# A graph-attention kernel whose odd adjacency halves are issued by another engine

## The reference, cut to what matters

```python
x: (8192, 256) f32;  adj: (8192, 8192) int32, 0 or 1, sparse, denser in the first rows and columns
h = x @ W                                             # W: 256 x 256
e = leaky_relu(s1[:, None] + s2[None, :], 0.2)        # s1 = h @ attn[:256, 0], s2 = h @ attn[256:, 0]
e = where(adj > 0, e, -9e15)
attention = softmax(e, axis=1)
out = layernorm(x + elu(attention @ h))
```

## Time and profile before

| what | value |
|---|---|
| median of 3 runs | 861.21 us (860.45 to 862.23) |
| the profiled execution's own time | 860.82 us |
| its span, first to last instruction | 859.1 us |
| moved by DMA | 320.21 MB |
| mean DMA rate over the span | 373 GB/s |
| busy: PE / DVE / ACT / POOL | 70% / 72% / 67% / 71% |
| granted TensorE clock, mean | 0.883 |

### The profile page before, as it was taken

The page is one execution under the profiler, slowest core; times in us unless marked ns, Lnnn a source line. Parts: engine busy times, 40 slices in busy tenths (PEclk is TensorE's granted clock), DMA queues, the critical chain, the costliest instruction groups (busy, mean ns, idle before and its releaser), DMA issues.

```text
span 859.1 us, 10648 instructions
## 1 busy us (share of the span) xinstructions
PE 598.4 (70%) x2590; PEld 385.8 (45%) x2633; DVE 614.6 (72%) x2385; ACT 577.6 (67%) x531; POOL 607.0 (71%) x695
## 2 busy tenths in 40 slices
PE   5588986646858777586787675777648775786641
PEld 4466662424536445353454343544425353454331
DVE  4257552567688987779897587788858877887863
ACT  3034536668777987878787497686959858897510
POOL 4487425778778777587865888888888786887742
PEclk9799999788978999898898988889889897999966
DMA  8999997999999999999999999999999998999400
GB/s 324 401 399 408 388 382 313 411 419 407 416 376 412 416 418 415 416 418 411 404 398 420 415 382 406 374 362 372 417 402 405 408 416 340 396 416 419 154 23 31
DMA packets 62850, 320.21 MB, mean 373 GB/s; under 512 B 19286, under 2 KB 37943, under 8 KB 46400
## 3 DMA queue, kind: packets, MB, share of 16 engines
q1 hardware_dynamic: 36176, 285.49, 81.7%
q0 software_dynamic: 25456, 29.79, 10.5%
q10 hardware_dynamic: 1152, 4.19, 1.2%
HBM read 344.79 MB, written 17.14 MB: 421 GB/s over the span
## 4 chain that ended last, share of the span: by engine, by line
issue 24%; POOL 20%; DMA 20%; DVE 17%; PE 15%; ACT 2%; POOLq 1%; SPq 0%; ACTq 0%; DVEq 0%
POOL GATH L1474 18%; DMA GATH<-haug,ids 7%; DMA ADJ<-in_adj_dram 6%; PE acc L513 6%; DMA WORK<-in_adj_dram,smalls 3%; DMA X<-in_x_dram 3%; PE pk L527 3%; PE acc L538 3%; DVE GATH L761 2%; ACT WORK L1296 2%; DVE diag L834 2%; PE mid_acc L604 1%; DVE smalls L775 1%; DVE WORK L951 1%; DVE PART L844 1%
## 5 line engine op out<-in xcount | busy, mean ns | idle before, releaser
L1474 POOL DMA_INDIRECT GATH<-haug,ids x448 | 471.5, 1053 | 132.5 <-issue 128.7
L1296 ACT ACTIVATE WORK<-ADJ 128x4096 bf16<-128x4096 int32 x128 | 461.9, 3609 | 138.7 <-PE pk L527 83.5
L527 PE MATMUL pk<-WORK,D 128*128 128x512 bf16 x981 | 256.6, 411 | 129.8 <-ACT WORK L1296 125.9
L527 PEld LDWEIGHTS pk<-WORK,D 128*128 128x128 bf16 x1024 | 100.1, 103 | 264.3 <-ACT WORK L1296 150.2
L538 PE MATMUL acc<-GATH,diag 128*128 128x256 f32 x512 | 157.3, 462 | 80.6 <-DVE diag L834 80.6
L538 PEld LDWEIGHTS acc<-GATH,diag 128*128 128x128 f32 x512 | 117.2, 235 | 123.6 <-DVE diag L834 99.2
L513 PE MATMUL acc<-Waug,GATH 128*128 128x258 f32 x256 | 64.8, 396 | 12.5 <-DVE GATH L761 12.5
L844 DVE SCALAR_TENSOR_TENSOR PART<-GATH,smalls,PART 128x256 f32<-128x256 f32 x128 | 62.2, 486 | 4.5
L770 DVE MAX8 smalls<-pk 128x8 f32<-128x512 f32 x64 | 44.5, 695 | 28.5 <-issue 28.2
L513 PEld LDWEIGHTS acc<-Waug,GATH 128*128 128x128 f32 x256 | 48.3, 196 | 24.9 <-issue 17.3
L604 PE MATMUL mid_acc<-X,WORK 128*128 128x256 f32 x256 | 58.0, 380 | 0.0
(11 more groups left out here) (180 smaller groups left out, 775.7 us busy)
## 6 DMA issues: line engine op xcount, KB each, us to landing
ADJ<-in_adj_dram SPq DMA_DIRECT2D x128, 2048.0 KB, 15.1
haug<-GATH POOLq DMA_DIRECT2D x32, 258.0 KB, 9.0
out_dram<-Y SPq DMA_DIRECT2D x32, 256.0 KB
GATH<-haug,ids POOLq DMA_INDIRECT x448
X<-in_x_dram SPq DMA_DIRECT2D x1, 4096.0 KB, 33.8
WORK<-in_adj_dram ACTq DMA_DIRECT2D x8, 512.0 KB
X<-in_x_dram SPq DMA_DIRECT2D x1, 3072.0 KB, 26.8
X<-in_x_dram SPq DMA_DIRECT2D x1, 1024.0 KB, 7.1
```

What stands on the lines that cost most here:

```text
L527: done = nc.tensor.matmul(pk[s % PKS][:], D16[:, k, :], A16[:, q % 2, k * BW:(k + 1) * BW], start=(half == 0 and k == 0), stop=(half == 1 ...
L1296: act.activation(A16[:, q % 2, :], ADJ[:, q % 4, :], ACT.Relu, scale=HALF_SCALE if q % 2 else 1.0, accum_out=degree[:, q // 2, q % 2:q % 2 ...
L1474: pool.indirect_dma_start(out=GATH[:, r, k * DA:(k + 1) * DA], out_offset=None, in_=haug, in_offset=bass.IndirectOffsetOnAxis(ap=ids[:, t ...
```

## The change

SP no longer issues the odd halves from q = 5 on. ScalarE issues them itself, half 2s + 3 directly behind count 2s (in the first stage as well as in the steps), having waited for the same count of `counted` as SP did. SP keeps halves 0 to 4, the even ones, X and the out stores. Nothing that is computed changes, and no slot, semaphore or byte is added.

```diff
             for q in range(4, HALVES):
-                load_half(q)
+                if q % 2 == 0:
+                    load_half(q)
                 for j in range(G):
                     if 2 * (pair_step(j) + 4) + 4 == q:
                         store(j)
...
+            def load_odd(q):
+                act.wait_ge(counted, q - 3)
+                act.dma_start(ADJ[:, q % 4, :], adj_tiles[:, q // 2, HW:2 * HW]).then_inc(adj_loaded[q % 4], 16)
+
             for q in range(2 * EARLY):
                 count(q)
+                if q % 2 == 0 and q >= 2:
+                    load_odd(q + 3)
             for s in range(EARLY, LAST + 1):
                 if s < T:
                     count(2 * s)
+                if s < T and 2 * s + 3 < HALVES:
+                    load_odd(2 * s + 3)
                 for x in chunk_at(s - 2):
                     mid_penalise(x)
                 if s < T:
```

## The result

| | before | after |
|---|---|---|
| median (lowest to highest, 4 runs) | 860.83 us (859.14 to 862.23) | 884.7 us (877.18 to 891.74) |
| the profiled execution's own time, span | 860.82 us, 859.1 us | 884.19 us, 882.5 us |
| mean granted TensorE clock | 0.883 | 0.873 |

The change makes the kernel slower: the ratio is 1.0249, 95% interval 1.0219 to 1.0278. One of the four executions after, 891.74 us, lies over 1.5% above the fastest and is left out of that ratio, which compares means; the median of the other three is 884.19 us. The forecast was 885.0 us.

A forecast was written before the change was run, and what follows sets the result against it. The prediction took the DMA engines' work to bound most of the span, with the gathers' way also without slack. Its terms, 4 - 3 + 17 + 6 = +24 us on 860.82 us, gave 885 us, range 859 to 915 us.

The forecast's parts named there:

- What bounds the kernel: Whole kernel: DMA engines' work for most of the span, with the way ids, gather, logits also without slack.
- Issue cost on ScalarE, 0: 62 added issues of about 0.38 us run beside ScalarE's counts: nothing, upper bound 24 us.
- Later issue, +4: Odd halves go out only when count 2s is dispatched, late at two long gaps: +4 us, bounds 0 and 20.
- No longer behind the stores, -3: Odd halves no longer queue behind SP's waits at its stores: -3 us, bounds 0 and -5.
- The third ring, +17: In the steps, a third full ring takes turns from the gathers, adding DMA idle time: 15 us plus 2 for restarts.
- Gathers landing 12 to 18 us after the last issue: Sign in the changed profile: gathers land 12 to 18 us after the last issue instead of 9.
- the much slower rival: The gathers' backlog becomes the bound, 13.0 instead of 10.95 us a step on the later half of tiles: 925 us, 15%.
- Chunks, +6: The second heavy group's eight chunk loads land later and ScalarE waits: +6 us; the first group's loads 0.
- DMA share of 0.95 to 0.98 in the steps: Sign in the changed profile: the DMA share in the steps falls to 0.95 to 0.98, from 1.01.
- The last load 20 us later with the tail unchanged: Sign at the end of the changed profile: last load some 20 us later, tail the same.
- The faster case: Odd halves freed from the stores decide, as both rings are seldom full together: 857 us, 12%.
- The case of no change: Same bytes, gains and idle times cancel or fall into slack: 861 us, 8%.

The follow-up runs named there:

- e5: The changed kernel with ScalarE issuing all halves from 4 on and the out stores too, on one ring: 869.42 us, ratio 1.0079.
- e1: The kernel before, all halves still on the sync engine's ring, odd halves waiting for one count more: 868.51 us, ratio 1.0082.
- e2: The changed kernel with ScalarE issuing each odd half earlier, directly behind count 2s - 1: 888.78 us, ratio 1.0296.
- e8: The changed kernel with halves in packets of 8 KB instead of 16 KB, on both rings: 864.89 us, ratio 1.0042.
- e7: The kernel before with halves in packets of 8 KB instead of 16 KB: 864.97 us, ratio 1.0038.
- e6: The kernel before with only the out stores moved to ScalarE, all halves left on the sync engine: 895.93 us, ratio 1.0414.
- e3: The kernel before with each out store one half later in the sync engine's order, behind the odd half: 866.84 us, ratio 1.006.
- e11: The kernel before with the out stores moved to ScalarE and halves in packets of 8 KB: 864.43 us, ratio 1.0041.

## Why the prediction was right, and where it was not

**What bounds the kernel: right.** More than half of the time lost is idle time of the DMA engines (12.3 of the 23.4 us), and the chain and the wait at the logits moved as said. Two places that the sum left at nothing hold much of the rest: the first stage (3.8 us at count 10) and the tail (3.6 us).

**Issue cost on ScalarE, 0: right.** The issue at 664.20 us has work on both sides of it, and e5 has twice as many and no loss in its steps.

**Later issue, +4: about the size of what e1 shows (+7, for a longer delay), but not where I put it.** I put it at the two long gaps at 121 and 147 us. In e1 half 16 is not late at all (-0.6 us). The change is 3.8 us late from half 6 to 13 with the first stage, and the +5.0 us at half 16 go with tile 0's gathers: the logits start at 160.81 us instead of 155.80, and 4 of the 5 us lie between the last gather's end and them (13.6 instead of 9.6). And e2 shows that none of the loss returns with an earlier issue. How much of the 24 us is this term, with two rings, stays open; nothing shows any, and e8 has the same late issues and is no slower than e7. The two issues themselves were late by more than taken, 14.7 and 15.1 us instead of some 10 (136.17 for 121.50, 162.17 for 147.06 us), yet the DMA share from 130 to 140 us only fell from 0.56 to 0.52.

**No longer behind the stores, -3: not seen.** e6 takes every half from behind the stores and has only a loss. e3 did not isolate it.

**The third ring, +17: the right cause, with one part of it missing.** I asked how often two rings of halves are full together and left the stores in the budget without asking whose turns they are. Of the 400 turns per tile, a store's packets are some 131 (in e6 27 stores with 8224 - 1152 packets on q10, the 1152 being the chunk loads, so 262 for two tiles), and on another ring than a half's they are turns taken together with it. That is worth 35 us by itself (e6), more than the whole change. In the change, even halves and stores still share a ring, so my sum came out near, partly by luck. With +4 not confirmed, -3 not seen, the chunks smaller than taken, and the first stage and the tail left at nothing, the terms do not stand one by one; how much of the 23.4 us is the ring's in the steps is not measured apart, and all that e8 shows is that smaller packets return 20 of 24.

Its two counts can be read in the thirds (120, 113 and 142) and in the turns. I had 304 turns for 367 packets (0.83), with the two rings full together for two thirds of q10's packets. By microsecond it is 0.93, with 4713 of q10's 9015 packets beside one of q1, so about half. (The 0.72 is to be set beside 256 for 367, 0.70, the case of always.) Fewer turns were lost than I took, while the idle time that they were to explain came out near (15 us summed, 12.3 measured), so the price of 255 packets per us of idle time does not hold with them.

**Gathers landing 12 to 18 us after the last issue: right**, median 16.6, though up to 30.5 at the tiles between 320 and 380 us. A step of 13.0 us on the last half of the tiles, the much slower rival, did not come: the lag grew in jumps (from 7.9 to 15.4 us between halves 48 and 56, from 12.7 to 19.0 between 80 and 88), and from half 88 to 127 by only 0.8 us, with swings of up to 6.3 us in between. As I had expected, the halves slow down, the rings empty, and the turns come back; the 4 us from 660 us on show it.

**Chunks, +6: half seen.** The first group's loads, now in a ring with odd halves, land in 6.5 us by the median on the page, so they hardly queue, and my 0 for them stands. The second group's waits fell, to three; the one of 10.29 us costs 2.3 us of idle DMA time (share 0.71 over 8 us). That is less than half of the 6.

**DMA share of 0.95 to 0.98 in the steps: partly.** 0.94 from 555 to 710 us, but 1.00 from 255 to 555 us, where the rate fell by 3% at an unchanged share. Why the same busy engines moved less there I can't say; for such a stretch GB/s tells more than the share.

**The last load 20 us later with the tail unchanged: nearly.** The last count starts 19.8 us later, but the tail grew by 3.6 us; I did not trace why.

**The rivals.** The faster case rested on both rings being full together less than a tenth of the time; about half of q10's packets run beside one of q1. The case of no change was that of the Trainium skill ("DMA: Bandwidth & Descriptors", Issuing engines are not separate DMA queues), by which the issuing engine changes the issue time alone. The measurement decides against it here: 884.7 us against 860.8 for the same bytes, and 895.9 for 32 small stores issued by another engine. The Trainium skill's other rule, the round by packets (Queues, rings and completion order), agrees with 205, 204 and 205 of the profile's packets.

## What to carry to other kernels

Before moving a DMA to another issuing engine, count packets by ring and ask which small-packet transfer lives on the turns of the large one: in these runs it got about one packet through per turn of the fullest ring. Keep large transfers, and small ones that have time, together on one ring if a latency-bound gather runs beside them, and cut the large packets when they must be on two. A wait that shrinks is no gain where the DMA engines are full: 40 us less of it brought nothing in e7. And look at the first stage too: in four kernels here, with halves on another ring beside the loads of X, the counts are 4 to 12 us late at half 8.

## What was not expected of the hardware

Moving only 32 stores of 256 KB, 8 MB of 320, to another ring costs 35 us (e6, 4.1%), more than moving 62 loads of 2 MB. Packets of 8 KB instead of 16 KB cost 3 us of 861 where they are not needed (e7) and return 20 and 31 us where they are (e8, e11).
